# A decoder kernel of two layers: the order of the steps of its first phase laid out anew on all five queues

## The chip, the cores and the metric

The kernel runs on one core of one Trainium2 chip. The time is the device time of one execution in microseconds (us). Before the change the median of three runs is 4827.91 us (4826.06 to 4829.62).

## The reference, cut to what matters

The input is x of shape 64 x 128 x 256 (64 sequences of 128 tokens) in float32, with a context of the same shape and two masks. Six blocks are added to x one after the other:

```
x = x + mamba(layernorm(x))                      # phase 1, chains M, V and N
x = x + cross_attention(layernorm(x), ctx, mask) # phase 1, chains Y and X
x = x + moe(layernorm(x))                        # shared part and router: phase 1, chain F
x = x + causal_attention(layernorm(x))           # phase 3
x = x + perceiver_attention(ctx, layernorm(x))   # phase 3
x = x + ternary_linear(layernorm(x))             # phase 3
```

Inside the mamba block the state recursion over 128 tokens with 32 heads is computed in closed form: with a cumulative sum c of A times dt over the tokens, head h needs the 128 x 128 matrix exp(c[t,h] - c[s,h]) times the masked product of B and C, and multiplies it with the tokens' values. The differences c[t,h] - c[s,h] of eight heads at a time are what the chain N calls "diff".

## The kernel before, in words

**Phases.** Phase 1 runs over the 64 sequences and does the first two blocks, the router and the shared part of the third. Phase 2 runs the 144 expert tiles. Phase 3 runs over the 64 sequences again and does the rest. The change touches phase 1 alone.

**Chains and steps.** In phase 1 the work is written as chains: M (first layer norm, dt, softplus series, cumulative sum), V (projections, convolution, gates) on sequence n, N (differences, exponentials, products with the state, output projection) on sequence n-1, Y and X (context keys and values, cross attention) on sequence n-2, F (router, shared expert, scatter) on sequence n-3. One body of the loop advances every chain by one sequence. Each chain is a Python generator on each engine and is cut into named steps by `yield`. The name of a step in the order is the chain's letter and the step's name: `Nd0` is step d0 of chain N.

**Order.** `ORDER[1]` lists for each of the five queues (SP, POOL, DVE, ACT, PE) in what order the steps of one body are issued. Nothing else orders them: every engine works strictly through its list, and waits (`done`) and reuse waits (`was`) on semaphores stand inside the steps. The buffers are single, so a step may not run before the reader of the same buffer in the body before has finished. A name that is listed but isn't a step of that engine (such as `Vgz` on PE) would be an error, so both orders hold the same steps.

**The steps that the prediction speaks of**, with their lines:

- On POOL (GpSimd): `Nd0` to `Nd3` (L618) subtract the per-token sums `cums` from the rows `Ew[j]`, 128x1024 each, in place. `Nm3` (L622) multiplies the fourth with the masked product `cbm`. `Mln1`, `Xln2`, `Fln3` (L582 to L585) are four instructions on 128x1 for the layer norms. `Msp` (L594 to L610) is thirteen small instructions for softplus; the last gives `a`. `Xx1r` (L635), `Nyg` (L625), `Nrms` (L628, L629), and `Fsc` (L646), which issues two scatter DMAs.
- On ACT (ScalarE): `Ng0` to `Ng3` (L1199) take the absolute value, `Ne0` to `Ne3` (L1202) the exponential. `Mln1`, `Xln2`, `Fln3` (L1145) normalise, `Mln1n`, `Xln2n`, `Fln3n` (L1137) copy the transposes out. `Mab` (L1171, L1173), `Frx` (L1257), `Vbc` (L1184), `Vxp` (L1187), `Xq` (L1241), `FhT` (L1263), and `Mcum` (L1178, L1179), which copies the cumulative sums to `cums` and `cumT`.
- On DVE (VectorE): `Nm0` to `Nm2` (L847) multiply the first three with `cbm`. `Ftop` (L893 to L905) is the top two of the router, `Fslot` (L908 to L912) the rows' places, `Msp` (L802 to L804) what POOL's `Msp` waits for, `Vcv` (L817) and `Vcv1` to `Vcv3` (L819) the convolution, `Ny0` and `Ny1` (L852) the state products' sum with the skip, `Xm0` to `Xm3` the maxima of the scores, `Xho` (L784, L785, L880) the heads' output, and bn_stats and bn_aggr (L754, L755) in `Mln1`, `Xln2`, `Fln3`.
- On PE (TensorE): `Mln1n`, `Xln2n`, `Fln3n` (L1402) transpose, `Fr` (L1390) the router's logits, `Vbc`, `Vip1`, `Vip1h`, `Xq` (L1390) projections, `Frk` (L1561, L1562), `Fgu` and `Fguh` (L1397), `Xs0` and `Xs2` (L1521, L1419), `Nv0` to `Nv3` (L1488), `Fdn` (L1390), `Mcum` (L1446, L1447), then the tail: `Xt0` to `Xt3`, `Vz`, `Xpv0` to `Xpv3`, `XOT`.
- On SP (SyncE, DMA issues): `Mco` (L437) stores `cumT` in memory, `Ncb0` to `Ncb3` (L446) fetch it back as eight heads' rows for all partitions, 512 KB each. `Ncb0` waits for the store of the body before. `Yc`, `Xm`, `Mx`, `Nx` fetch inputs, `Fm` (L464) and `Fo` (L467) store.

So one ring runs from body to body: `Mcum` (PE) makes the sums, `Mcum` (ACT) copies them, `Mco` (SP) stores them, `Ncb0` fetches them, `Nd0` (POOL) of the next body starts, and later in that body POOL's `Msp` makes the `a` for the next `Mcum`.

The waits of the ring in the code:

```
if j == 0:
    done(sp, "cum_out", b, 16)          # Ncb0 on SP
was(sp, "Yk", b, j + 1)
...
done(pool, f"wide{j}", b, 16)           # Nd0 to Nd3 on POOL
...
done(pool, "ratio", b)                  # Msp on POOL, for DVE's Msp
...
done(pe, "a", b)                        # Mcum on PE
```

Of the kernel before, what the change touches and what calls it, by code (L numbers as in the profile page):

```python
# [47 lines left out]
ORDER = {  # L48
    1: {
        "SP": """  # L50
            Ncb0 Ncb1 Ncb2 Yc Xm Mx Ncb3 Nx Mco Fm Fo
        """,
        "POOL": """
            Nd0 Nd1 Nd2 Xx1r Fln3 Xln2 Mln1 Nd3 Msp Nm3 Fsc Nyg Nrms
        """,
        "DVE": """
            Fln3 Xln2 Nm0 Mln1 Fr Yk Ftop Mdt Fslot Msp Xm0 Xm1 Fhg Nm1 Nm2 Xm2 Xm3 Fxo Vcv Vcv1 Vcv2 Vcv3 Ny0 Vxs2 Ny1 Vcb Vxdt Vgz Nx1 Xho
        """,
        "ACT": """
            Ng0 YcT Ne0 Ng1 Fln3 Xln2 Fln3n Xmr Xln2n Mln1 Frx Mln1n Xq Mab Vbc Ne1 Ng2 Yv Fth Ne2 Ng3 FhT Ne3 Xm0 Xm1 Vxp Xm2 Mcum Xm3 NYt0 Xt0 NYt1 Xt1 Vcth Xt2  # L60
            Xt3 Nsq XOT NyT Vtz
        """,
        "PE": """
            YcT Yk Nv0 Fln3n Yv Xln2n Fr Mln1n Xq Vbc Mdt Frk Xs0 Fgu Fguh Vip1 Vip1h FhT Xs2 Fdn Mcum Nv1 Nv2 Xt0 Nv3 Xt1 Ny0 Xt2 VCB Ny1 Xt3 Xpv Xpv0 VxsT Xpv1
            Xpv2 NyT Xpv3 Vz Vzh Npr Nprh XOT
        """,
    },
    3: {
# [1752 lines left out]
```

How the kernel before makes its waits and increments, by code:

```python
        def done(eng, name, b, k=1):  # L124
            eng.wait_ge(SEM[name], at(name, b, k))
# [1 line left out]
        def was(eng, name, b, k=1):  # L127
            if not isinstance(b, int) or b > 0:
                eng.wait_ge(SEM[name], at(name, b, k) - PER[name])
# [202 lines left out]
        def link(eng, name, b, ins, bare=False):  # L333
            steps[name] += 1
            assert steps[name] <= links[name], name
            ins.then_inc(SEM[f"link_{name}"], 1)
            eng.wait_ge(SEM[f"link_{name}"], at(f"link_{name}", b, steps[name]))
            if bare:
                eng.sem_inc(SEM[f"passed_{eng.engine.name}"], 1)
# [28 lines left out]
        def met(eng, me, k):  # L369
            eng.sem_inc(SEM[f"phase_{me}"], 1)
            for other in ("PE", "DVE", "ACT", "POOL"):
                if other != me:
                    eng.wait_ge(SEM[f"phase_{other}"], k)
# [18 lines left out]
        @block.sync  # L393
# [67 lines left out]
            def F(b):  # L461
                yield "m"
                done(sp, "slot", b)
                tell(sp.dma_start(rows(slot_d, b), meta[:, :]), "meta_out", 16)
                yield "o"
                done(sp, "xo", b)
                tell(sp.dma_start(rows(x2_d, b), xo), "xo_out", 16)
            program(sp, "SP", 1, (("M", M, 0), ("N", N, 1), ("Y", Y, 2), ("X", X, 2), ("F", F, 3)))
            sp.wait_ge(SEM["plan"], 1)
            sp.dma_start(routed_d[SPARE:SPARE + P, :], zero).then_inc(SEM["tails"], 16)
            zeros_behind(sp, range(NE // 2))
            sp.wait_ge(SEM["scattered"], at("scattered", NB, 0))
```

## Time and profile before

| | |
|---|---|
| median of three runs | 4827.91 us |
| the profiled execution's own time | 4827.89 us |
| its span, first to last instruction | 4826.3 us |
| PE busy | 4224.3 us (88%) |
| DVE busy | 3368.1 us (70%) |
| ACT busy | 2909.1 us (60%) |
| POOL busy | 2734.9 us (57%) |
| mean granted clock of TensorE | 0.923 of full |

Busy shares are means over three phases of different kinds. Phase 1 reaches to about 2430 us, phase 2 to about 2850 us, phase 3 to the end. A granted clock of 1.00 is 2.4 GHz, 0.50 is 1.2 GHz. PE rows give matmuls, PEld rows weight loads beside them; SPq rows are DMA issues. A float32 matmul shows as two records.

### The profile page before, as it was taken

The numbers are of one execution on the slowest core, as the hardware profiler recorded it, in microseconds if no ns is written. First come the engines' busy times: TensorE is split into PE (matmuls) and PEld (weight loads), VectorE is DVE, ScalarE is ACT, GpSimd is POOL, SyncE is SP. The second block draws the span as 40 slices with busy tenths as digits, with TensorE's granted clock in tenths as the row PEclk, the third lists the DMA queues.
The fourth block names the chain that finished last, engine by engine and source line by source line (L and its number), as shares of the span: only waits on it lengthen the run. The fifth ranks groups of instructions, "written<-read, shape, count | busy, mean of one in ns | idle before, by whom it ended". The sixth has DMA issues, their size and how long they took to land.

```text
span 4826.3 us, 119218 instructions
## 1 busy us (share of the span) xinstructions
PE 4224.3 (88%) x33430; PEld 3093.7 (64%) x33431; DVE 3368.1 (70%) x8668; ACT 2909.1 (60%) x7030; POOL 2734.9 (57%) x4093
## 2 busy tenths in 40 slices
PE   3788888888888888888869979999999999999998
PEld 2666666666666666666647756666666666666665
DVE  2776677666776667766745547777777777777776
ACT  2666666666666666666634436666666666666564
POOL 3666666666666666666622235555555555555554
PEclk9888888888888888888979989999999999999998
DMA  5222222222222222222214411111111111111110
GB/s 155 72 82 90 74 74 74 89 83 74 74 78 92 75 74 74 83 88 75 74 59 145 144 39 31 30 31 31 31 29 31 30 31 31 31 31 31 31 31 18
DMA packets 215885, 304.09 MB, mean 63 GB/s; under 512 B 56608, under 2 KB 167456, under 8 KB 215840
## 3 DMA queue, kind: packets, MB, share of 16 engines
q1 hardware_dynamic: 188864, 240.33, 16.0%
q0 software_dynamic: 19200, 52.45, 3.3%
q10 hardware_dynamic: 7776, 10.75, 0.7%
q8 instruction: 23, 0.38, 0.0%
q14 instruction: 22, 0.18, 0.0%
HBM read 239.19 MB, written 64.23 MB: 63 GB/s over the span
## 4 chain that ended last, share of the span: by engine, by line
PE 51%; POOL 20%; issue 17%; DVE 6%; ACT 2%; POOLq 1%; SPq 1%; DMA 0%; DVEq 0%; ACTq 0%
PE Q L1397 14%; PE Q L1402 8%; POOL arena L618 7%; PE Q L1390 6%; PE Q L1488 4%; PE Q L1425 3%; PE Q L1735 3%; PE Q L1768 3%; PE Q L1589 3%; PE Q L1434 2%; POOL arena L625 2%; PE Q L1601 2%; POOL arena L605 1%; PE Q L1419 1%; POOL arena L606 1%
## 5 line engine op out<-in xcount | busy, mean ns | idle before, releaser
L1402 PE MATMUL Q<-ident,arena 128*128 128x128 f32 x4768 | 801.5, 291 | 148.7 <-ACT arena L1145 35.3
L1402 PEld LDWEIGHTS Q<-ident,arena 128*128 128x128 f32 x4768 | 557.0, 145 | 388.2 <-issue 123.7
L1397 PE MATMUL Q<-Wkvl,arena 128*128 128x512 f32 x1024 | 500.3, 601 | 0.0
L618 POOL TENSOR_TENSOR arena<-arena 128x1024 f32<-128x1024 f32 x256 | 479.4, 1889 | 7.2 <-DMA arena<-cum_rows 7.2
L682 POOL TENSOR_TENSOR l<-l,half_pow 128x8 f32<-128x8 f32 x192 | 318.5, 1659 | 233.2 <-DVE l L1025 231.3
L707 POOL TENSOR_TENSOR arena<-arena,part_of 128x512 f32<-128x512 f32 x256 | 263.7, 1041 | 190.8 <-DVE part_of L1063 190.4
L1488 PE MATMUL Q<-arena 128*16 128x128 f32 x4096 | 223.6, 339 | 169.1 <-DVE arena L847 167.9
L769 DVE TENSOR_REDUCE mx<-Q 128x4 f32<-128x512 f32 x512 | 343.9, 681 | 10.2 <-PE Q L1419 5.5
L1425 PEld LDWEIGHTS Q<-ident,arena 128*128 128x128 f32 x2048 | 244.2, 148 | 116.5 <-issue 84.9
L1425 PE MATMUL Q<-ident,arena 128*128 128x128 f32 x2048 | 314.0, 288 | 1.3 <-ACT arena L1155 0.4
L1155 ACT ACTIVATE arena<-Q,mx 128x128 f32<-128x128 f32 x1024 | 281.8, 372 | 0.7 <-DVE mx L769 0.5
L1419 PE MATMUL Q<-arena 32*128 32x128 f32 x4096 | 278.7, 274 | 0.0
L1162 ACT ACTIVATE arena<-Q 128x512 f32<-128x512 f32 x384 | 222.0, 597 | 83.2 <-PE Q L1425 79.1
L1488 PEld LDWEIGHTS Q<-arena 128*16 128x16 f32 x4096 | 129.4, 107 | 222.2 <-DVE arena L847 169.0
L1202 ACT ACTIVATE arena<-arena 128x1024 f32<-128x1024 f32 x256 | 268.4, 1048 | 0.1
L1199 ACT ACTIVATE arena<-arena 128x1024 f32<-128x1024 f32 x256 | 268.3, 1048 | 0.0
L1419 PEld LDWEIGHTS Q<-arena 32*128 32x128 f32 x4096 | 261.4, 188 | 3.6
L1361 ACT ACTIVATE arena<-Q,mxl 128x256 f32<-128x256 f32 x512 | 235.4, 472 | 45.0 <-DVE mxl L1058 37.6
L1390 PEld LDWEIGHTS Q<-arena,Win 128*128 128x128 f32 x1536 | 235.8, 235 | 33.5 <-issue 29.2
L1434 PE MATMUL Q<-arena 128*17 128x128 f32 x4096 | 208.1, 276 | 41.4 <-ACT arena L1162 41.4
L1390 PE MATMUL Q<-arena,Win 128*128 128x128 f32 x1536 | 236.9, 315 | 3.1 <-ACT arena L1184 2.2
L1397 PEld LDWEIGHTS Q<-Wkvl,arena 128*128 128x128 f32 x1024 | 170.3, 191 | 104.2 <-issue 104.0
(310 smaller groups left out, 10753.3 us busy)
## 6 DMA issues: line engine op xcount, KB each, us to landing
arena<-cum_rows SPq DMA_DIRECT2D x256, 512.0 KB, 6.1
arena<-routed_rows SPq DMA_DIRECT2D x144, 128.0 KB, 2.1
expert_rows<-arena POOLq DMA_DIRECT2D x144, 128.0 KB, 2.0
arena<-in_x_dram SPq DMA_DIRECT2D x128, 128.0 KB, 4.4
arena<-in_ctx_dram SPq DMA_DIRECT2D x128, 128.0 KB
x_rows<-arena SPq DMA_DIRECT2D x128, 128.0 KB, 1.7
arena<-x_rows SPq DMA_DIRECT2D x128, 128.0 KB, 2.3
out_dram<-arena SPq DMA_DIRECT2D x64, 128.0 KB, 1.7
```

The lines of the kernel that those rows point to most:

```text
L618: tell(g.tensor_tensor(E8[j], E8[j], cums[:, 8 * j:8 * j + 8].unsqueeze(2).broadcast_to([P, 8, T]), ALU.subtract), "diff")
L682: link(pool, c, b, g.tensor_tensor(l2[:, k, :], l2[:, k, :], half_pow[:, :], ALU.pow), bare=True)
L769: largest = v.tensor_reduce(mx[:, 4 * j:4 * j + 4], pj, AX.X, ALU.max, negate=True)
L1155: last = s_.activation(S[:, j, g, :], banks[j][:, g * T:(g + 1) * T], ACT.Exp, bias=mx[:, 4 * j + g:4 * j + g + 1])
L1202: tell(s_.activation(Ew[j], Ew[j], ACT.Exp, scale=-1.0), "E")
L1390: last = mm(out, lhs(c), rhs(c), start=c == 0, stop=c == n - 1)
L1397: last = mm(out, lhs(c), rhs(c), start=c == 0, stop=c == n - 1)
L1402: last = nc.tensor.transpose(out[:, c * P:(c + 1) * P], src[:, c * P:(c + 1) * P], ident[:, :])
L1419: last = mm(banks[j][:, g * T:(g + 1) * T], QT[r, g, :], KT[r, g // 2, :], start=False, stop=g == NG - 1)
L1425: last = nc.tensor.transpose(bank[:, g * T:(g + 1) * T], S[:, j, g, :], ident[:, :])
L1434: last = mm(bank[32 * (h % 4):32 * (h % 4) + AW + 1, h // 4 * T:(h // 4 + 1) * T], V[:, h, :], PT[:, j, g, :], start=True, stop=True)
L1488: last = mm(Q[3 + j // 2][32 * (i % 4):32 * (i % 4) + HP, (h // 4 % 4) * T:(h // 4 % 4 + 1) * T], xdt[:, h * HP:(h + 1) * HP], E8[j][:, i, :],
```

## The change

Only the lists of phase 1 change. No step is added or removed, and no step's own code changes; the same instructions are issued in another order on each of the five queues.

- SP: `Fm` (the store of the rows' places) moves ahead of `Mco`.
- POOL: `Nd3` moves up to stand right behind `Nd0`, `Nd1`, `Nd2`; then come `Xx1r`, `Mln1`, `Fln3`, `Xln2`. `Nm3` moves ahead of `Msp`, `Nyg` ahead of `Fsc`.
- DVE: `Mln1` first; `Nm1` and `Nm2` move up; `Ny0` and `Ny1` move up, in between `Xm0` and `Xm1`; the convolution moves up ahead of the score maxima and is cut in two halves; `Nx1` ahead of `Vxdt`, `Xho` last.
- ACT: `Ng0`, `Ne0` to `Ne3` and the norms are interleaved anew, `NYt0`, `NYt1` and `Nsq` move up, `Yv` moves down.
- PE: `Mln1n`, `Mdt`, `Nv1` move up, `VCB`, `Nv2`, `Nv3`, `Ny0`, `Ny1` too, `NyT` and `Npr`; `Xs2` moves down behind `Mcum`, and the tail becomes `Xt0 VxsT Xt1 Xt2 Vz Vzh Xt3 Xpv ... XOT`.

```diff
     1: {
         "SP": """
-            Ncb0 Ncb1 Ncb2 Yc Xm Mx Ncb3 Nx Mco Fm Fo
+            Ncb0 Ncb1 Ncb2 Yc Xm Mx Ncb3 Nx Fm Mco Fo
         """,
         "POOL": """
-            Nd0 Nd1 Nd2 Xx1r Fln3 Xln2 Mln1 Nd3 Msp Nm3 Fsc Nyg Nrms
+            Nd0 Nd1 Nd2 Nd3 Xx1r Mln1 Fln3 Xln2 Nm3 Msp Nyg Fsc Nrms
         """,
         "DVE": """
-            Fln3 Xln2 Nm0 Mln1 Fr Yk Ftop Mdt Fslot Msp Xm0 Xm1 Fhg Nm1 Nm2 Xm2 Xm3 Fxo Vcv Vcv1 Vcv2 Vcv3 Ny0 Vxs2 Ny1 Vcb Vxdt Vgz Nx1 Xho
+            Mln1 Fln3 Nm0 Xln2 Yk Nm1 Mdt Nm2 Fr Ftop Fslot Msp Vcv Vcv1 Xm0 Fhg Ny0 Ny1 Xm1 Fxo Vcv2 Xm2 Vcv3 Xm3 Vxs2 Vcb Nx1 Vxdt Vgz Xho
         """,
         "ACT": """
-            Ng0 YcT Ne0 Ng1 Fln3 Xln2 Fln3n Xmr Xln2n Mln1 Frx Mln1n Xq Mab Vbc Ne1 Ng2 Yv Fth Ne2 Ng3 FhT Ne3 Xm0 Xm1 Vxp Xm2 Mcum Xm3 NYt0 Xt0 NYt1 Xt1 Vcth Xt2
-            Xt3 Nsq XOT NyT Vtz
+            Ng0 Ne0 YcT Ng1 Ne1 Ng2 Mln1 Ne2 Mln1n Ng3 Fln3 Ne3 Fln3n Mab Frx Xln2 Vbc Xmr NYt0 Vxp Xln2n Xq Fth NYt1 Xm0 FhT Nsq Mcum Xm1 Yv NyT Xm2 Vcth Xm3 Xt0
+            Xt1 Xt2 Vtz Xt3 XOT
         """,
         "PE": """
-            YcT Yk Nv0 Fln3n Yv Xln2n Fr Mln1n Xq Vbc Mdt Frk Xs0 Fgu Fguh Vip1 Vip1h FhT Xs2 Fdn Mcum Nv1 Nv2 Xt0 Nv3 Xt1 Ny0 Xt2 VCB Ny1 Xt3 Xpv Xpv0 VxsT Xpv1
-            Xpv2 NyT Xpv3 Vz Vzh Npr Nprh XOT
+            YcT Yk Yv Nv0 Mln1n Mdt Nv1 Fln3n Fr Vbc Xln2n Vip1 Vip1h Frk VCB Xq Fgu Fguh Xs0 Nv2 Nv3 Ny0 Ny1 FhT Fdn Mcum Xs2 NyT Npr Nprh Xt0 VxsT Xt1 Xt2 Vz
+            Vzh Xt3 Xpv Xpv0 Xpv1 Xpv2 Xpv3 XOT
         """,
     },
```

## Rows read from the trace of the kernel before

**Rows 1.** The page, part 1: busy us, share of the span, instructions
```profile
PE 4224.3 (88%) x33430; PEld 3093.7 (64%) x33431; DVE 3368.1 (70%) x8668; ACT 2909.1 (60%) x7030; POOL 2734.9 (57%) x4093
```

**Rows 2.** Instructions of one line, L629, which runs once in each body
```profile
L629 POOL TENSOR_TENSOR ss<-ss,half_pow x61: 567/567/572, 175.4 to 2427.2; 128x1 f32<-128x1 f32 x61
```

**Rows 3.** Timeline of POOL in one body: start us, us, engine line, what
```profile
1039.24 5.59 POOL L618 TENSOR_TENSOR arena<-arena 128x1024 f32<-128x1024 f32 x3
1045.53 0.73 POOL L635 TENSOR_TENSOR arena<-arena,bv0b 128x256 f32<-128x256 f32 x1 [0.69 <-DVE arena L880]
...
1058.85 0.24 POOL L594 TENSOR_TENSOR arena<-arena 128x32 f32<-128x32 f32 x1 [6.12 <-DVE arena L804]
...
1062.25 1.20 POOL L605 TENSOR_TENSOR arena<-arena 128x32 f32<-128x32 f32 x1 [0.34 <-POOL arena L602]
...
1066.18 0.26 POOL L610 TENSOR_TENSOR arena<-arena,Aneg 128x32 f32<-128x32 f32 x1 [0.18 <-POOL arena L609]
1066.40 2.41 POOL L622 TENSOR_TENSOR arena<-arena 128x1024 f32<-128x1024 f32 x1
```

**Rows 4.** Timeline of ACT in the same body
```profile
1048.37 0.60 ACT L1145 ACTIVATE arena<-arena,mvF 128x256 f32<-128x256 f32 x1 [2.04 <-POOL mvF L585]
...
1057.78 1.05 ACT L1202 ACTIVATE arena<-arena 128x1024 f32<-128x1024 f32 x1
...
1067.98 0.25 ACT L1179 ACTIVATE arena<-Q 32x128 f32<-32x128 f32 x1
```

**Rows 5.** Timeline of SP's queue, end of that body
```profile
1068.39 0.35 SPq L437 DMA_DIRECT2D cum_rows<-arena  x1
...
1071.06 1.33 SPq L446 DMA_DIRECT2D arena<-cum_rows  x3
```

**Rows 6.** Landings of L446's later fetches, bodies from 1108.6 and 1146.1
```profile
DMA to landing us min/median/max: 6.0/6.5/7.0
...
DMA to landing us min/median/max: 4.6/5.2/5.7
```

**Rows 7.** Timeline of DVE in the same body
```profile
1052.98 0.17 DVE L893 RECIPROCAL rt<-rt 128x1 f32<-128x1 f32 x1
...
1055.73 0.14 DVE L905 TENSOR_SCALAR meta<-rt 128x1 f32<-128x1 f32 x1
...
1062.13 2.41 DVE L847 TENSOR_TENSOR arena<-arena 128x1024 f32<-128x1024 f32 x2
...
1065.99 3.23 DVE L817 SCALAR_TENSOR_TENSOR arena<-arena,convw,convb 128x128 f32<-128x128 f32 x4
1069.25 3.55 DVE L819 SCALAR_TENSOR_TENSOR arena<-arena,convw 128x128 f32<-128x128 f32 x12
```

**Rows 8.** Timeline of PE in the same body
```profile
1054.73 1.75 PE L1390 MATMUL Q<-arena,Win 128*128 128x128 f32 x8
...
1056.82 0.39 PE L1521 MATMUL Q<-mrow,mask_w 32*128 32x512 f16 x2
...
1058.08 1.98 PE L1397 MATMUL Q<-Wsgu,arena 128*128 128x512 f32 x4
1059.90 1.95 PE L1390 MATMUL Q<-arena,Win 128*128 128x128 f32 x16
...
1063.85 1.13 PE L1390 MATMUL Q<-Wsd,arena 128*128 128x256 f32 x4
1066.49 0.64 PE L1446 MATMUL Q<-arena,triu 128*128 128x32 f32 x2 [1.51 <-POOL arena L610]
...
1070.14 0.63 PE L1488 MATMUL Q<-arena 128*16 128x128 f32 x16
```

**Rows 9.** Stages: start:end us, busy us of each engine, granted clock, DMA
```profile
1046.00:1048.20 2.20, 0.00 (x0) 0.00 (x0) 1.89 (x6) 0.33 (x1) 1.80 (x5) 1.00 0.01 2
1049.00:1056.00 7.00, 6.68 (x28) 6.10 (x29) 2.73 (x16) 3.79 (x11) 3.42 (x7) 0.53 0.00 0
...
1066.70:1069.50 2.80, 2.80 (x37) 1.85 (x38) 2.77 (x3) 1.61 (x7) 2.63 (x2) 0.50 0.02 6
```

## The prediction

> **What bounds the kernel now.** I read the page first, then one line's instructions for the loop's pace, then the timeline of one body engine by engine, then the stages with their clock. On the page no engine is full over the whole span [rows 1], which says little, since three phases are mixed. The pace says more: L629 runs once in a body, its 61 instructions lie between 175.4 and 2427.2 us [rows 2], so a body of phase 1 takes (2427.2 - 175.4)/60 = 37.53 us. The median of the runs (4827.91) and the profiled execution (4827.89) are one number here, and the span lies 1.6 us below it, so a sum over bodies can be added to either.
>
> In one body the reader should see a ring. With POOL's first difference at 1039.24 as zero: ScalarE's `Fln3` starts at 9.1 [rows 4]; POOL waits 6.1 us for VectorE's L804 and starts `Msp` at 19.6; its last instruction L610 ends at 27.2 [rows 3]; TensorE waited 1.5 us for just that and makes the sums [rows 8]; ScalarE's copy L1179 ends at 29.0 [rows 4]; the store is issued at 29.15, the first fetch at 31.8 [rows 5], and the next body starts at 37.5. No engine is full; each waits for another once or twice around the ring. So the place to read this change is when `cumT` is copied, counted from the body's first difference.
>
> Two things in this body stretch it. **The clock:** with no matmul from 1046.0 to 1048.2, TensorE then runs at 0.53 for 7 us (0.50 is 1.2 GHz), and again at 0.50 after the wait of 1.5 us ahead of `Mcum` [rows 8, 9]. Sixteen 128-column records take 1.95 us at 2.4 GHz, eight take 1.75 at 1.2 [rows 8]. **VectorE and POOL hold each other up:** POOL's L605, 128x32, takes 1.20 us (its sisters L609 and L610 some 0.26) while VectorE's L847 runs; POOL's L622 takes 2.41 where L618 of the same shape takes 5.59/3, and in that time VectorE's four L817 take 3.23 us where twelve L819 take 3.55 [rows 3, 7]. Each has two operands in SBUF. They take turns, an instruction at a time.
>
> **The change, part by part.** Nothing is added or removed, so each term is a move. All times below are after `Nd0`.
>
> 1. POOL: four differences take 4 x 1.87 = 7.5 us instead of 5.6, then `Xx1r` 0.7: 8.2. The fetches come 1.3 us apart at best (512 KB at the 400 GB/s they reach, an estimate from the landings in [rows 6]), so the fourth is in time.
> 2. `Mln1` on POOL is the next thing ScalarE needs. Uncontended it is 1.3 us, done at 9.5. But VectorE finishes the body before only at about 6.3 (step 7), runs two bn_stats pairs (0.7 each), and then `Nm0`, 1.2 us [rows 7], from 7.75 to 9.0, with both operands in SBUF. I charge 0.75 us: 10.2. The two other norms meet `Nm1` and `Nm2` in the same way.
> 3. ScalarE is in order: `Mln1` 0.6, `Ne2` and `Ng3` about 0.95 each in a row (1.05 shown, starts 0.94 apart [rows 4]), with the copy `Mln1n` between: `Fln3` starts at 12.95 instead of 9.1. This is what the row of differences costs: `Ng3` stands ahead of `Fln3`.
> 4. From there `Ne3` (0.95) stands ahead of the copy `Fln3n`, done 14.75; then the logits at the low clock (0.9, half of `Vbc`'s eight records), maximum and exponential 0.7 with the hand-offs (an estimate, by the small instructions of 0.2 to 0.3 in [rows 3, 7]), done 16.4, `Ftop` 2.9 us (1052.98 to 1055.87 [rows 7]) and 0.3 for a collision with POOL's `Nm3`: 19.6.
> 5. `Frk` stands behind `Vbc` and the two `Vip1`. `Vbc` costs 1.75 at 1.2 GHz [rows 8]; ScalarE's copy lets `Vip1` start at 18.0; it takes 1.95 us at 2.4 GHz, 3.5 at 1.2. TensorE has four gaps of about 1 us between 9.5 and 15, so I let the clock be low until about 18.5: `Vip1h` ends 20.5, `Frk` 20.7, then `Fslot` 1.0 and VectorE's `Msp` 0.8. POOL's `Msp` starts at 22.5, against 19.6. It no longer meets L847: 7.55 us less 0.95 and 0.75 is 5.85. Now it meets `Vcv` and `Vcv1` instead, eight operations of 0.3; I add 0.75: `a` at 29.1, against 27.2.
> 6. But TensorE isn't there. Behind `Frk` it does `VCB` (after ScalarE's 0.5 copy, 0.9 together), `Xq` 1.15, `Fgu` 1.8, `Xs0` 1.25, `Nv2`, `Nv3`, `Ny0`, `Ny1` 0.57 each with 0.1 of waiting, `FhT`, a copy and `Fdn` 2.0 [rows 8], starts taken one from the next: 20.7 + 9.5 = 30.2. `Mcum` 0.9 and the copies 0.45 end at 31.55. **Term: 31.55 - 29.0 = +2.55 us.** Before, `Mcum` waited for `a`; now it waits for TensorE's own list, and the products and state transposes put ahead of it are 2.4 of that.
> 7. The tail: 11.2 us of matmuls behind `Mcum` with waits of about 2 us for the softmax and for `Vxdt` put `XOT` at 44.1 and `Xho` at 45.6, that is 6.3 into the next body: the assumption of step 2. Its cover is thin: if the tail ends 1 us later, `Mln1` on VectorE is late by as much.
> 8. SP: `Fm` ahead of `Mco` is 0.6 us in a queue that waits for `cumT` anyway: nothing. If `Fslot` were later than `cumT` it would cost, but it is 10 us earlier. `Fo` behind `Mco` is issued while SP waits for the store.
> 9. The way through memory. Store and first fetch: 2.8 us from the copy's end [rows 4, 5]. The first fetch's landing is not shown. The second and third land 4.6 to 7.0 us after they are issued [rows 6], and they are issued 0.7 us and more behind the first; taking off the 1.3 us of its successor, the first lands 4.1 to 5.5 us after its issue. So the copy gates the next `Nd0` after 6.9 to 8.3 us; the body before uses 8.5, so it has 0.2 to 1.6 us of slack there. The scatter's transfers end before the fetches now, where they overlapped, so I take the lower half: 7.4.
>
> **The sum:** 31.55 + 7.4 = 38.95 us a body, against 37.53: +1.42. Times 63 bodies from one first difference to the next of 64 sequences: +89 us. 4827.9 + 89 = 4917 us. Phases 2 and 3 don't change. `Nsq`, `NYt0`, `NYt1`, `Yv`, `Nx1`, `NyT` cost nothing by themselves, covered by ScalarE's and VectorE's waits ahead of `Mcum`; if that cover were gone, each is 0.3 to 0.6.
>
> On the clock, the second fall came after a gap of 1.5 us only [rows 8, 9]. The Trainium skill, page "TensorE: Matmul & The Clock Gate", section "HAM oscillation — how this bites in real kernels", says that only a long gap without matmuls brings the clock down; by that rule the gaps of step 5, none of them above 1.3 us, would leave it at 2.4 GHz. Its result is the second rival.
>
> **The rivals.**
>
> - *The clock stays high* (chance 0.12). The gaps of step 5 are short, and TensorE is busy through step 7. Then `Fr` and `Vbc` take half, `Vip1h` ends at 19.4, `Ftop` becomes the later one, and the ring shortens by 1.05: 37.9 us, +23 us, 4851. Against it: 1.5 us sufficed in [rows 8, 9]. The page's rule named above is this case.
> - *Faster: the ring is tight only if both charges fall on it* (0.24). Place: from POOL's `Mln1` to ScalarE's `cumT`. If neither the clock (1.05) nor the turn-taking with `Nm0` (0.75) lies on the ring, `cumT` is copied at 29.75, and with the fetch at its fastest, 7.0, the body is 36.75: -0.78 x 63 = -49, 4779. It decides from a copy that ends before about 30.5. For it: POOL's wait of 6.1 us has gone, the scatter is out of the fetches' way, and `Msp` no longer meets L847. Against it: the ring has little give, since ScalarE alone has six steps ahead of `Fln3n`.
> - *The ring is bound elsewhere, in the same time* (0.10). If `Nd0` is not gated by the fetch but POOL's order again, the moves cancel, 4820 to 4837.
> - *Low clock to the end of `Vip1h`* (0.08). 3.5 us instead of 2.5, and `Nm0` holding up `Nd3` as well: 40.2 us, +168, 4996.
>
> The forecast has what is left, 0.46.
>
> **How the numbers follow.** About 0.2% (10 us) is what a measurement of this kernel can tell from no change. Faster 0.24, within it 0.10, slower 0.46 + 0.12 + 0.08 = 0.66. The unknown costs are the clock (0 to 2 us a body), the turns on SBUF (0 to 1.5) and the landing (6.9 to 8.3); the forecast's own range is 37.9 to 39.8 us, 4851 to 4971. The full range reaches to the faster rival, 4778, and up to 4995.
>
> **What would show it.** Right: L629's spacing near 38.9 us; ScalarE's first L1145 3 to 4 us later behind `Nd0`; POOL's L594 at 22 to 23 and its wait gone to ahead of `Nd0`, put down to `cum_rows` or an issue; TensorE's L1446 no longer waiting for L610; a low clock between 11 and 19. L605 near 0.25, and some of the centre instructions near 1 us beside L847. Wrong: L1446 starting before 28, or L1446 still waiting for L610, or `Nd0` following L629 without idle time, which would say that the ring isn't closed by the memory round trip.

## The result, and the profile after

The changed kernel takes 4888.43 us (median of four runs, 4870.07 to 4907.4), the kernel before 4826.99 (median of four): a ratio of 1.013, with a 95% interval of 1.0086 to 1.0174. It is 61 us slower, where 89 were forecast. The profiled execution is the slowest of the four, 4907.4 us, and lies 79 us above the profiled execution of the kernel before; the numbers of its bodies and rings below are from that trace. One run of a later kernel (5030.45 us, in "All together") lies over 1.5% above the fastest of its kernel, at a lower clock, and is left out of that kernel's median.

Page of the changed kernel, parts 1 and 4 (shares of the chain that ended last):

```profile
PE 4195.5 (86%) x33430; PEld 3034.8 (62%) x33431; DVE 3296.0 (67%) x8668; ACT 2914.5 (59%) x7030; POOL 2744.1 (56%) x4093
...
PE 72%; ACT 11%; issue 8%; DVE 4%; POOL 2%; DMA 2%; SPq 1%; DVEq 0%; ACTq 0%; POOLq 0%
```

The same line of the kernel before:

```profile
PE 51%; POOL 20%; issue 17%; DVE 6%; ACT 2%; POOLq 1%; SPq 1%; DMA 0%; DVEq 0%; ACTq 0%
```

POOL had 20% of the last chain; now it has all but left it. The loop's pace, the row that answers to [rows 2]:

```profile
L629 POOL TENSOR_TENSOR ss<-ss,half_pow x61: 567/567/574, 178.7 to 2497.2; 128x1 f32<-128x1 f32 x61
```

(2497.2 - 178.7)/60 = 38.64 us a body, against 37.53. The mean hides something that the kernel before doesn't have. The bodies of that one, from one first difference to the next, are nearly all alike: 55 of the 56 from the fifth to the sixtieth are under 37.8 us and none is over 38.5. Of the same 56 of the changed kernel 21 are under 37.8, near 37.55, and 29 are over 38.5, up to 40.6.

Timeline of POOL, one body of the changed kernel of 40.6 us (start us, us, what, then idle time before it and who ended it), answering to [rows 3]:

```profile
1033.42 5.61 POOL L618 TENSOR_TENSOR arena<-arena 128x1024 f32<-128x1024 f32 x3 [3.85 <-DMA arena<-cum_rows]
...
1042.55 0.73 POOL L635 TENSOR_TENSOR arena<-arena,bv0b 128x256 f32<-128x256 f32 x1 [1.12 <-DVE arena L880]
...
1050.24 2.35 POOL L622 TENSOR_TENSOR arena<-arena 128x1024 f32<-128x1024 f32 x1 [0.45 <-ACT arena L1202]
1059.27 0.28 POOL L594 TENSOR_TENSOR arena<-arena 128x32 f32<-128x32 f32 x1 [6.68 <-DVE arena L804]
...
1062.93 0.25 POOL L605 TENSOR_TENSOR arena<-arena 128x32 f32<-128x32 f32 x1 [0.34 <-POOL arena L602]
...
1065.14 0.25 POOL L610 TENSOR_TENSOR arena<-arena,Aneg 128x32 f32<-128x32 f32 x1 [0.18 <-POOL arena L609]
```

`Nd0` now stands idle 3.85 us for its fetch; in [rows 3] and [rows 5] POOL went from one body into the next without a wait. The wait of 6 us ahead of L594 has stayed. L605, 1.20 us in [rows 3], takes 0.25, now that VectorE's L847 doesn't run beside it.

Timeline of ACT, then of SP's queue, then of PE, in the same body, answering to [rows 4, 5, 8]:

```profile
1039.76 0.60 ACT L1247 ACTIVATE arena<-Q 128x512 f32<-128x512 f32 x1 [0.72 <-PE Q L1434]
1040.25 1.05 ACT L1199 ACTIVATE arena<-arena 128x1024 f32<-128x1024 f32 x1
...
1048.54 0.59 ACT L1145 ACTIVATE arena<-arena,mvF 128x256 f32<-128x256 f32 x1
...
1067.49 0.25 ACT L1179 ACTIVATE arena<-Q 32x128 f32<-32x128 f32 x1
```

```profile
1067.90 0.35 SPq L437 DMA_DIRECT2D cum_rows<-arena  x1
...
1069.84 1.58 SPq L446 DMA_DIRECT2D arena<-cum_rows  x3
```

```profile
1050.41 1.03 PE L1390 MATMUL Q<-Wr,arena 128*128 128x16 f32 x4 [0.78 <-ACT arena L1137]
1051.28 2.06 PE L1390 MATMUL Q<-arena,Win 128*128 128x128 f32 x8
...
1053.80 3.52 PE L1390 MATMUL Q<-arena,Win 128*128 128x128 f32 x16
...
1066.57 0.30 PE L1446 MATMUL Q<-arena,triu 128*128 128x32 f32 x2
```

ScalarE's work on the differences starts at 1040.25, right behind `XOT` of the tail (L1247), though POOL's first difference ended near 1035.3. `Fln3` starts 15.1 us behind `Nd0` (mean of the bodies 14.0), where it was 9.1. L1446 no longer waits for L610: over 114 records the view of that line names no idle time. In the kernel before it named this, over 118 records:

```profile
  POOL arena L610: 202.3, 118
```

`Vip1` and `Vip1h` take 3.52 us where they took 1.95, at the low clock.

Stages (start:end us, us, busy us of PE, PEld, DVE, ACT, POOL, clock, DMA), answering to [rows 9]:

```profile
1049.50:1053.00 3.50, 2.72 (x14) 2.60 (x13) 1.01 (x5) 2.05 (x7) 2.64 (x2) 0.58 0.00 0
1053.00:1056.50 3.50, 3.45 (x16) 3.05 (x16) 1.61 (x11) 1.16 (x3) 0.00 (x0) 0.50 0.00 0
1056.50:1067.00 10.50, 9.24 (x90) 6.69 (x88) 8.42 (x25) 4.87 (x12) 5.44 (x15) 0.98 0.01 0
```

For the ring as a whole I took from each trace the starts of a few lines, counted from the end of the copy to `cumT` (L1179) and averaged over 56 bodies:

```
us behind the copy's end      before   after
Nd0 starts (L618)              8.61     6.29
Xho's sum starts (L880)       14.40    14.03
router's maximum (L889)       21.70    22.98
Fslot starts (L908)           26.36    28.27
next copy ends                37.54    38.60
```

From the tail to the router's maximum the new order loses 1.65 us (7.30 to 8.95), on to `Fslot` 0.63, and it wins 0.85 behind that and 0.37 ahead of it: 1.06 in sum.

These are means over rings that differ. From one copy to the next, 22 of the 56 rings of the changed kernel take 37.57 us, as long as in the kernel before (37.54). Sorted by how much of a ring TensorE spent at 1.2 GHz:

```
us at 1.2 GHz   rings   us from copy to copy, mean
3.4             22      37.57
6.8             26      38.92
10.2             2      39.88
13.7             6      40.55
```

One ring each with 3.4, 6.8 and 13.7 us (start:end us, us, busy us of PE, PEld, DVE, ACT, POOL, clock, DMA):

```profile
1608.20:1645.76 37.56, 29.35 (x264) 21.65 (x262) 24.91 (x71) 24.58 (x54) 23.95 (x37) 0.95 0.24 79
1067.74:1106.58 38.84, 30.86 (x264) 22.79 (x262) 24.87 (x71) 24.69 (x55) 23.98 (x37) 0.91 0.21 76
1948.84:1989.34 40.50, 33.65 (x264) 25.20 (x262) 24.59 (x71) 24.81 (x54) 24.32 (x37) 0.83 0.22 73
```

What the other 34 rings take above 37.57 adds up to 58 us, which is nearly the whole loss of this execution's loop. It stands where the further low clock stands: in the tail (`Xho` starts 14.91 us behind the copy in the 16 rings with low clock there, 13.69 in the 40 without), and between `Xho` and `Fslot`.

### The profile page after: what moved, and what is told of

It reads as the page before. It is cut to its first block, busy times and chain, and to the rows that moved or that the text cites. A ratio compares the mean times of both kernels' runs of the same rounds, so it can differ in the third digit from the quotient of the medians.

```text
span 4905.7 us, 119223 instructions
## 1 busy us (share of the span) xinstructions
PE 4195.5 (86%) x33430; PEld 3034.8 (62%) x33431; DVE 3296.0 (67%) x8668; ACT 2914.5 (59%) x7030; POOL 2744.1 (56%) x4093
## 4 chain that ended last, share of the span: by engine, by line
PE 72%; ACT 11%; issue 8%; DVE 4%; POOL 2%; DMA 2%; SPq 1%; DVEq 0%; ACTq 0%; POOLq 0%
PE Q L1397 21%; PE Q L1390 15%; PE Q L1402 11%; ACT arena L1199 4%; PE Q L1419 3%; PE Q L1434 3%; PE Q L1425 3%; PE Q L1735 3%; PE Q L1768 3%; PE Q L1589 3%; ACT arena L1202 2%; PE Q L1488 2%; PE Q L1601 1%; DMA arena<-cum_rows 1%; POOL arena L618 1%
## 5 line engine op out<-in xcount | busy, mean ns | idle before, releaser
L1402 PE MATMUL Q<-ident,arena 128*128 128x128 f32 x4768 | 801.0, 289 | 183.5 <-ACT arena L1145 45.8
L1402 PEld LDWEIGHTS Q<-ident,arena 128*128 128x128 f32 x4768 | 543.4, 144 | 443.5 <-issue 145.7
L618 POOL TENSOR_TENSOR arena<-arena 128x1024 f32<-128x1024 f32 x256 | 480.3, 1900 | 272.2 <-DMA arena<-cum_rows 270.9
L1390 PE MATMUL Q<-arena,Win 128*128 128x128 f32 x1536 | 318.5, 384 | 3.8 <-ACT arena L1184 0.9
L1425 PEld LDWEIGHTS Q<-ident,arena 128*128 128x128 f32 x2048 | 246.4, 143 | 114.6 <-issue 101.0
L1390 PEld LDWEIGHTS Q<-arena,Win 128*128 128x128 f32 x1536 | 290.0, 287 | 30.0 <-ACT arena L1184 29.2
L1425 PE MATMUL Q<-ident,arena 128*128 128x128 f32 x2048 | 282.1, 276 | 3.4 <-ACT arena L1155 2.4
L1361 ACT ACTIVATE arena<-Q,mxl 128x256 f32<-128x256 f32 x512 | 235.4, 472 | 45.0 <-DVE mxl L1058 37.6
L819 DVE SCALAR_TENSOR_TENSOR arena<-arena,convw 128x128 f32<-128x128 f32 x768 | 238.6, 372 | 2.4
L847 DVE TENSOR_TENSOR arena<-arena 128x1024 f32<-128x1024 f32 x192 | 235.2, 1225 | 2.2 <-ACT arena L1202 2.2
L1397 PE MATMUL Q<-Wout,arena 128*128 128x256 f32 x512 | 158.2, 463 | 86.4 <-ACT arena L1214 85.7
```

What stands on the lines that cost most here:

```text
L618: tell(g.tensor_tensor(E8[j], E8[j], cums[:, 8 * j:8 * j + 8].unsqueeze(2).broadcast_to([P, 8, T]), ALU.subtract), "diff")
L1390: last = mm(out, lhs(c), rhs(c), start=c == 0, stop=c == n - 1)
L1397: last = mm(out, lhs(c), rhs(c), start=c == 0, stop=c == n - 1)
L1402: last = nc.tensor.transpose(out[:, c * P:(c + 1) * P], src[:, c * P:(c + 1) * P], ident[:, :])
L1425: last = nc.tensor.transpose(bank[:, g * T:(g + 1) * T], S[:, j, g, :], ident[:, :])
```

## The experiments

Twelve kernels were run, each in turns with the kernel before on the same chip; the ratio is to that. The changed kernel itself was not run again beside them. Its four runs spread over 37 us, so a difference to its 4888.43 us says little when it is below about 25 us. Times inside a body are of the profiled execution.

**A longer way through memory, in the changed kernel.** The edit, on SP in `Ncb0`, with an array `again_d` beside `cum_d`:

```diff
 done(sp, "cum_out", b, 16)
+tell(sp.dma_start(rows(again_d, b), cumT[0:NH, :]), "again", 16)
+done(sp, "again", b, 16)
```

> The changed kernel with a second store of cumT, to another array, issued and waited for on SP between the first store and the first fetch: about 2 us more on the way through memory in each body. Theory M (of the prediction: the ring is closed by the memory round trip, since POOL's Nd0 stands idle 3.9 us for cum_rows in a body): +2 us x 63 = +126 us, about 5015. Theory R (read in the trace after: the ring runs through the in-order lists of TensorE and ScalarE, Ng0 on ScalarE starts only behind the body before's XOT, 6.8 us after Nd0 starts, so 4.9 us of the trip are slack): within 20 us of the changed kernel's 4888.

It took 5019.95 us (ratio 1.0401, with the 95% interval 1.0384 to 1.0419), 132 over the changed kernel. Theory M's 5015 was met, though partly by luck: it charged 2 us a body, and the fetch came only 1.5 later. The first fetch was issued 3.6 us behind the copy instead of 2.1, the first difference started 7.7 behind it instead of 6.3, and a body took 40.48 us instead of 38.60. Theory R, read straight from the chain of waits, fell. `Ng0` starts late, and so the chain doesn't name POOL, but POOL's four differences end at 6.29 + 7.76 = 14.05 us behind the copy, and `Xho`, the other thing that `Xx1r` waits for, ends at 14.65 on the mean, and later than the fourth difference in all 56 bodies. Two rings of nearly one length meet at `Xx1r`; the chain of waits shows the later one. They are also tied by more than that wait. `Xho`'s sum L880, 0.43 us in the kernel before, takes up to 1.6 in the changed kernel and up to 2.2 with the longer way, when POOL's L618 runs beside it. So of the delay of 1.40 us ahead of `Nd0` 1.26 reach `Xx1r`. The body grew by 1.88, since the low clock rose too, from 6.3 us a body to 10.1.

**The same in the kernel before.**

> The kernel before with the same second store and wait on SP ahead of the first fetch: the fetch is issued 1.5 us later, as the trace of the first such run shows. The changed kernel took 132 us for it. If the kernel before is closed through memory just as tightly, as the prediction had it with 0.2 to 1.6 us of slack: 0 to 80 us, somewhere near the middle (+40). If it has the whole slack that the trace of the changed kernel lets one expect (a first fetch lands 4.2 us after its issue there, so 7.0 after the copy, against 8.6 used): under 15 us. As much as the changed kernel, 100 us or more: then the memory ring is no difference between the two.

4833.7 us, 1.0012 (1.0002 to 1.0022), 8 us. Here the first fetch was issued 5.1 us behind the copy instead of 2.8, a longer delay than in the changed kernel, but `Nd0` started only 0.5 later (9.1 behind the copy instead of 8.6). The idle time of POOL (its waits between 200 and 2300 us: us in total, times, longest) of the changed kernel, of the changed kernel with the longer way, and of the kernel before with the longer way:

```profile
POOL arena L618 <- DMA arena<-cum_rows: 226.7, 80, 4.3
```

```profile
POOL arena L621 <- DMA arena<-cum_rows: 302.7, 96, 5.8
```

```profile
POOL arena L621 <- DMA arena<-cum_rows: 39.8, 78, 1.1
```

So the kernel before had about 1.8 us of slack in its memory ring, and the changed one has next to none: of its 1.5 us, 1.4 reached `Nd0`. This is the sharpest difference between the two: one edit, 8 us in the one and 132 in the other.

**ScalarE's norms ahead of its row.** In the changed kernel's ACT list:

```diff
-Mln1n Ng3 Fln3 Ne3 Fln3n Mab Frx
+Mln1n Fln3 Ng3 Fln3n Mab Ne3 Frx
```

> The changed kernel with two swaps on ScalarE: Fln3 ahead of Ng3, and Fln3n and Mab ahead of Ne3. Theory R: the chain of waits has Ng3 (1.05 us) and Ne3 (0.95) ahead of the router's logits, so a body is up to 1.9 us shorter, less what POOL's Fln3 (done 0.9 us earlier than ScalarE takes it) and the later Nm3 give back: -1 us x 63, about 4825. Theory M, with the row of differences as the cost: the same sign, through cumT, but no less idle time of POOL ahead of Nd0.

4912.0 us (1.0189, 1.017 to 1.0208), where 4825 was expected: a miss. It is 24 above the changed kernel's median, but the two profiled executions are alike (4905.5 and 4907.4 us, a body 38.64 and 38.60), so what is shown is that nothing was gained. `Ne3` later makes POOL's `Nm3` later (17.1 us behind `Nd0` instead of 15.7) and POOL's `Msp` behind it too (24.1, 23.8 before the edit). `Fln3` itself came only 0.4 us earlier (13.6 behind `Nd0`).

**VectorE's `Msp` early.** In the changed kernel's DVE list:

```diff
-Nm2 Fr Ftop Fslot Msp Vcv
+Nm2 Fr Msp Ftop Fslot Vcv
```

> The changed kernel with VectorE's Msp ahead of Ftop instead of behind Fslot: POOL's Msp can start some 6 us earlier and a is ready some 5 us earlier. Theory R: Mcum on TensorE is held by TensorE's own list (it starts 1.2 us after a is ready), so nothing moves but POOL's idle time: within 20 us of 4888. Rival (POOL's Msp still on the ring, or its turns with the convolution on SBUF cost VectorE): 1 us a body or more, under 4825.

4895.18 us (1.0151, 1.0134 to 1.0168), 7 over the changed kernel and inside its spread. `a` was ready at 24.8 us behind `Nd0` instead of 30.0, and `cumT` was copied at 32.2 instead of 32.3. POOL's wait of 6 us, the longest in its view, was worth nothing.

**The row undone.** In the changed kernel's lists of POOL and ACT, all else as changed:

```diff
-Nd2 Nd3 Xx1r Mln1 Fln3 Xln2 Nm3
+Nd2 Xx1r Mln1 Fln3 Xln2 Nd3 Nm3
...
-Mln1n Ng3 Fln3 Ne3 Fln3n Mab Frx Xln2 Vbc Xmr NYt0
+Mln1n Fln3 Fln3n Mab Frx Xln2 Ng3 Vbc Xmr Ne3 NYt0
```

> The changed kernel with the row of differences undone: POOL's Nd3 back behind the three norms, and ScalarE's Ng3 and Ne3 behind Fln3n, Frx and Xln2. Theory T (two rings are tied within 0.7 us at POOL's Xx1r: the memory trip with four differences, and TensorE's tail with Xho; behind it the norms wait for the row and for Ng3 and Ne3): the router's maximum comes 1.3 to 1.9 us earlier behind Xho, a body is about 1 us shorter, 4888 - 63 = about 4825, the time of the kernel before. Rival (as ScalarE's two swaps alone, which gave 4912: what ScalarE gains there, POOL's Msp loses behind the later Nm3): 4880 to 4920.

4838.41 us (1.0017, 1.0008 to 1.0027): 50 of the 61 us are back. From copy to copy all 56 rings are alike, 37.56 us on the mean, each with 6.8 us of low clock, always between `Xho` and the end of `Vip1` and never in the tail. So undoing the row took away the long rings; against the changed kernel's 22 rings of 37.57 us it won nothing. On the means the pieces moved like this: the tail is 1.2 us shorter (`Xho` starts 12.84 behind the copy), from `Xho` to the router's maximum it is 8.47 us instead of 8.95, on to `Fslot` 5.92 instead of 5.29, where the low clock now always lies, and 10.33 behind that in both. `Fln3` starts 12.2 us behind `Nd0` instead of 14.0, and 1.3 of these 1.8 us are the earlier `Xho`. The part for which step 3 blamed the row, `Ng3` ahead of `Fln3`, is thus 0.5 us.

Of the 1.2 us in the tail the clock explains only 0.3, since the changed kernel's rings with a high clock throughout it stand at 13.69. The rest shows right behind the copy. `NyT` (PE's L1402) starts 0.6 us behind it in both kernels, at the high clock, but ScalarE's L1214, which waits for it, starts 1.3 us behind the copy in all rings here and 2.0 in 55 of 56 of the changed kernel. Two rows of the changed kernel (copy at 724.09), two of this one (copy at 698.28):

```profile
724.69 0.66 PE L1402 MATMUL Q<-ident,arena 128*128 128x128 f32 x4
726.07 0.60 ACT L1214 ACTIVATE arena<-Q 128x512 f32<-128x512 f32 x1 [1.20 <-PE Q L1402]
...
698.89 0.66 PE L1402 MATMUL Q<-ident,arena 128*128 128x128 f32 x4
699.58 0.60 ACT L1214 ACTIVATE arena<-Q 128x512 f32<-128x512 f32 x1 [0.52 <-PE Q L1402]
```

What holds it up there is not shown.

**`Mcum` early as well.** To the early `Msp` comes, on PE and ACT of the changed kernel:

```diff
-Xs0 Nv2 Nv3 Ny0 Ny1 FhT Fdn Mcum Xs2
+Xs0 Mcum Nv2 Nv3 Ny0 Ny1 FhT Fdn Xs2
...
-Xq Fth NYt1 Xm0 FhT Nsq Mcum Xm1
+Xq Fth Mcum NYt1 Xm0 FhT Nsq Xm1
```

> The changed kernel with VectorE's Msp ahead of Ftop (alone: 4895, no change) and Mcum on TensorE directly behind Xs0, on ScalarE behind Fth: cumT is copied some 5 us earlier, and the first fetch is issued when Fo lets it, 2 to 2.5 us earlier. Theory T: the memory ring gets slack, but TensorE's list is as long and Xho as late, 0.5 to 0.7 us are left to gain by POOL's Xx1r, 4845 to 4880, and POOL's idle time for cum_rows shrinks from 4 us to about 2. Theory M (memory ring alone): -2 us x 63, 4760.

4859.06 us (1.0054, 1.0037 to 1.0071), 29 under the changed kernel, in the interval of theory T. The copy ended at 28.2 us behind `Nd0`, 4.1 earlier, but the first fetch was issued at 33.4, 1 us earlier only, since on SP it stands behind `Fo`, which waits for `xo`. The low clock, 7.0 us a body, lies outside the tail in nearly every ring, as with the row undone; 53 of the 56 rings take 37.58 us on the mean. How much of the 29 us is the clock and how much the earlier `Mcum` is not separated.

**Extra matmuls in front of waits.** A helper on PE writes to a part of a bank that nobody reads then, in front of the waits of `Yk`, `Mdt`, `Fr`, `VCB`, `Npr` and `Vz`:

```diff
+def fill(n, bank=4):
+    for _ in range(n):
+        mm(Q[bank][:, 0:64], ident[:, :], ones[:, 0:64], start=True, stop=True)
...
+fill(3)
 done(pe, "ln1_T", b)
```

> The changed kernel with three extra 128x64 float32 matmuls in front of each of six waits of TensorE (Yk, Mdt, Fr, VCB, Npr, Vz), into a bank that nobody reads then, to keep TensorE busy. Theory: the bodies of 39 to 40.6 us are those with 7 to 14 us at 1.2 GHz, those of 37.6 have 3.4 us; with the clock high all the time a body is 36.5 to 37.5 us: -1.2 us x 63, about 4810, and no body over 38. Rival (the clock is a companion of the longer waits, not their cause, or the extra matmuls cost more than they hide): 4888 or slower.

4840.95 us (1.0028, 1.0016 to 1.0041): 47 less than the changed kernel, with eighteen matmuls more. 47 of 56 bodies are under 37.8 us, three over 38.5; low clock is 3.3 us a body instead of 6.3, and none of it in the tail. Nothing but TensorE's activity was changed, so the clock makes the long bodies; it doesn't just go with them. And the row of differences still stands in this kernel: undoing the row brought back 50 us and keeping the clock up 47, so the two are not separate costs. The row costs mainly through the low clock. How the order brings the clock down more often is not shown.

**More of them.**

> The changed kernel with more extra matmuls than the 18 of the run at 4841 (29 in nine places): there every body had one stretch of 3.4 us at 1.2 GHz, 16 us after Nd0, and took 37.5; the six bodies without it took 37.0. If the clock is what is left: no low stretch, 36.9 us a body, about 4800. If the extra matmuls cost as much as they give: 4841 or slower.

4862.64 us (1.0063, 1.0035 to 1.0091, runs from 4845 to 4883): the second half of the expectation. But the bodies tell more than the median. 36 have no low clock at all and take 36.84 us, 17 have 10 us of it and take 40.43. The same instructions in the same order, 3.6 us apart with nothing but the clock to tell them apart. What tips a body over I can't say.

**The same on the kernel before**, nine ahead of `Nv0`'s wait and six ahead of `Mcum`'s:

> The kernel before with nine extra 128x64 float32 matmuls ahead of Nv0's wait and six ahead of Mcum's, where it stands idle 2.6 and 1.5 us and then has 6.8 and 3.4 us at 1.2 GHz in every body. If the low clock is on its ring: 1.5 to 2.5 us a body, 4670 to 4735. If its ring runs through POOL, VectorE and the memory trip with TensorE's matmuls beside them: under 30 us gained, or none.

4824.21 us (0.9983, 0.9973 to 0.9993), 6 us under the kernel before in the same rounds. The expectation's second half fits the median. The trace doesn't fit it: it is of the fastest of the ten runs, 4803.58 us, 24 us under the profiled execution of the kernel before, and its low clock fell from 9.8 to 3.8 us a body. In it 12 of the 56 rings have no low clock and take 35.58 us, 26 have 3.4 us of it and take 37.26, and 18 have 6.8 and take 38.14. Two in a row, one with 6.8 us and one without (start:end us, us, busy us of PE, PEld, DVE, ACT, POOL, clock, DMA):

```profile
946.12:984.25 38.13, 33.01 (x297) 25.16 (x289) 26.34 (x69) 24.21 (x55) 24.61 (x37) 0.91 0.26 78
984.25:1019.52 35.27, 30.24 (x297) 23.86 (x289) 25.88 (x73) 24.31 (x55) 22.91 (x36) 1.00 0.26 84
```

So the low clock does lie on the ring of the kernel before, 1.7 us for the first 3.4, and a version of it that kept the clock up in every body would be some 2 us a body faster than it is (an estimate from these rings, 35.58 against 37.54). The extra matmuls did that in one ring of five; in the others they moved the low clock into the tail, 6 to 10 us behind the copy, where it costs. This is the only version of the twelve with an interval under the kernel before, by an amount below the 0.2% that I set as the bound.

**All together**, the row undone, `Msp` and `Mcum` early, and on POOL `Msp` ahead of `Nm3`; without extra matmuls, and with 25 of them:

> The row undone (alone 4838) together with VectorE's Msp ahead of Ftop and Mcum behind Xs0 (together alone 4859, 29 under the changed kernel), and POOL's Msp ahead of Nm3. Theory: both rings get shorter, the two gains of 50 and 29 us add: about 4809, or more than that since cumT is copied some 3 us before the tail needs it. Rival (both only took away the same 0.7 us at POOL's Xx1r, and the low clock of 6.8 us in each body holds the pace at 37.55): 4825 to 4840.

> The same with 25 extra 128x64 float32 matmuls ahead of eight waits of TensorE. In the row undone alone every body has 6.8 us at 1.2 GHz, in which Vbc and both Vip1 run in 5.6 us instead of 3. If they are on the ring and the extra matmuls keep the clock up: 2 us a body less, about 4690 to 4710, under both kernels. If the clock falls in some bodies all the same, as in the run at 4863: around 4780 and a wide spread.

4960.12 us (1.0282, 1.0257 to 1.0307) and 4845.1 (1.0037, 1.0023 to 1.0051). Both expectations failed, the first on the other side. Two causes show in the trace of the first. One is the clock: 27 bodies without low clock take 37.5 us, and eleven with 15 us of it take 42.9. The other is in these pieces of the chain of waits of a body without low clock (start us, us, what):

```profile
1301.45 1.14 DVE arena L802
1302.62 0.36 DVE arena L803
...
1307.37 1.15 DVE arena L817 x4
...
1308.54 3.34 DVE arena L819 x4
```

and in POOL's timeline beside it:

```profile
1300.65 1.89 POOL L618 TENSOR_TENSOR arena<-arena 128x1024 f32<-128x1024 f32 x1
...
1309.32 2.40 POOL L622 TENSOR_TENSOR arena<-arena 128x1024 f32<-128x1024 f32 x1
```

L802, 128x32, is 0.19 us in the changed kernel and 1.14 here, behind POOL's L618, which ends at 1302.54. `Vcv1`, four L819 in 1.46 us in the changed kernel, takes 3.34, one of the four 2.45, while POOL's `Nm3` runs. Moved together the steps put both collisions, 2.8 us, on the chain of waits. With the 25 extra matmuls the clock is 1.00 in the loop and a body is 37.56 us, the two collisions still in it. Whether `Nm3` ahead of `Msp` would have brought this version under the kernel before was not tried.

**The row undone with the extra matmuls.**

> The row undone alone with the same 25 extra matmuls: tells whether Msp and Mcum early matter once the clock is up. If the memory ring is then the tighter one: about 0.5 to 1 us a body more than with them, 4720 to 4760. If not: the same time.

4851.96 us (1.005, 1.0036 to 1.0065), 14 slower than without them. The clock is high in nearly the whole loop, and still the tail is 1.3 us longer (`Xho` 14.15 us behind the copy instead of 12.84). Part of that may be the extra matmuls in it; ScalarE's L1214 also starts late again, 2.5 to 2.6 us behind the copy instead of 1.3 in 51 of 56 rings. The two were not separated. Against the version with all moves and the same extra matmuls it is 7 us slower, with intervals that overlap: that fits the second half of the expectation, "the same time", though both times lie above the 4690 to 4760 that were expected.

## Why the prediction was right, point by point

The direction and the range were right, and the size was 1.4 times too large. The sum came near for the wrong reasons. In the 22 rings without further low clock the copy ends 31.30 us behind `Nd0`, 2.4 later than before (2.55 forecast), and `Nd0` starts 6.27 behind the copy, 2.3 earlier than before (1.1 forecast): 37.57 us, and nothing lost. The loss is the further low clock in the other 34 rings, which the sum, with its one low stretch of the same cost in every body, doesn't have. With the memory leg as measured it would have come to 31.55 + 6.27 = 37.82 us a body, some 18 us for the kernel. That the time fell near the forecast is in good part luck.

- **The sum to the copy** (step 6): forecast 31.55 us behind `Nd0`, measured 32.31 on the mean and 31.30 in the 22 rings. `Mcum` held by TensorE's own list: right, it starts 1.2 us behind the end of `a` and names no wait, and with `a` 5 us earlier nothing moved.
- **The tail** (step 7): from copy to `XOT` and `Xho` 45.6 - 31.55 = 14.05 forecast to its end, 14.65 measured.
- **The way through memory** (step 9), the mis-sized term: forecast 7.4 us from copy to `Nd0`, measured 6.29. The first fetch is issued 2.1 us behind the copy where it was 2.8: `Fm` ahead of `Mco`, which step 8 put at nothing, left only `Fo` between store and fetch. It lands about 4.2 behind its issue, against some 4.6 in the sum. So `Nd0` starts earlier than the tail allows anything to follow, `Xho` ends 8.4 us into the body instead of 6.3, and step 2 starts late. The ring is not closed by memory alone, as step 9 has it; it is tied between memory and tail within 0.6 us. A memory leg of the forecast's length would not have given the forecast's body: with the longer way it was 7.7 us, and a body took 40.48.
- **The row of differences** (step 3) as the main cost: right that it is what loses, as undoing it brings back 50 of 61 us, but not by the way step 3 has it. `Fln3` starts 14.0 us behind `Nd0` (12.95 forecast, 9.1 before), of which 2 us are the late `Xho`; with the row undone it still starts at 12.2, and 0.5 us is the row's own part. The 22 rings have the whole row and lose nothing. The row costs where it comes with more low clock.
- **The clock** (step 5): low, but from about 16 us to 19.4 or 22.4, not from 11 to 18.5, and in 16 of 56 rings in the tail as well. I charged 1 us to every body. In truth 22 rings pay nothing against the kernel before, 26 pay 1.35 us on the mean and the rest 2.3 to 3. The rival in which the clock stays high is refuted for the changed kernel, whose largest gap on TensorE is 1.56 us. Its forecast of 37.9 didn't hold either: with the extra matmuls the rings without low clock take 36.9 and 36.7. The rule that the prediction takes from the page "TensorE: Matmul & The Clock Gate" of the Trainium skill, section "HAM oscillation — how this bites in real kernels", is one on long gaps without matmuls. It didn't hold here: the body of the rows above, with no gap over 1.4 us, had three stretches at 1.2 GHz, and the measurement decides.
- **The turns on SBUF**: `Msp` on POOL at 6.1 us instead of 7.6, forecast 6.6. VectorE's `Vcv` and `Vcv1` together take 2.6 us. The 0.75 us between `Nm0` and POOL's `Mln1` came to 0.5: POOL's four instructions take 1.85 us in every body, of which the last takes 0.69 instead of 0.19 in the body shown.
- **The signs**: a body 38.64 us (38.9 forecast), POOL idle ahead of `Nd0` for `cum_rows`, L1446 without a wait for L610 and L605 at 0.25 us came as foretold. L594 came at 23.8, not 22 to 23, its wait of 6 us was not gone but stayed beside the new one, `Fln3` came 4.9 us later and not 3 to 4, and the low clock lay later than 11 to 19.
- **The rival of the other side** needed the copy before 30.5 us; it came at 32.3 on the mean and 31.1 at the earliest.

With the row undone and all the rest in place, the state products early among it, the kernel stands at 1.0017 of the kernel before, 8 us. That is what the rest costs without the row; what it costs beside the row no run shows.

## What to carry to other kernels

When a step moves up, ask for each queue what then stands behind it: here one 1.9 us instruction on GpSimd and its two on ScalarE went ahead of the norms on which the next stage waits, and undoing that brought back most of the loss. But look at single bodies before you name the cost. The mean body hid that 22 of 56 lost nothing and the others lost by TensorE's clock, and eighteen extra matmuls brought back as much as undoing the move. Two rings of nearly one length hide each other in a chain of waits, which shows only the later; a delay put in on purpose, in both kernels, tells what slack each has. And gains of single moves do not add: two moves worth 50 and 29 us, together with one more, were 122 slower than the better of them.

## What the runs showed of the hardware

- TensorE's clock fell although no gap in the changed kernel's loop was over 1.56 us, and identical bodies took 36.84 us without and 40.43 with 10 us of low clock. Extra matmuls in front of waits kept it up and won 47 us in the one kernel (26 with more of them) and 6 in the other, and lost 14 in a third.
- The kernel before spends more of its loop at 1.2 GHz than the changed one (9.8 against 6.3 us a body) and is faster: it matters where the low clock lies. The page "TensorE: Matmul & The Clock Gate" of the Trainium skill, section "Terms", counts the penalty as the low time's missing share of clock. By that 3.4 us cost 1.7 (an estimate from the page), and in the kernel before with extra matmuls they did, 37.26 us against 35.58. But rings of 37.5 to 37.6 us have 10.2 us of low clock in the kernel before, 6.8 with the row undone and 3.4 in the changed kernel.
- VectorE and GpSimd take turns by whole instructions when both have two operands in SBUF: 128x128 in 2.45 us instead of 0.34, 128x32 in 1.14 instead of 0.19, and 128x256 (L880) in up to 2.2 instead of 0.43.
- Several versions with different orders and clocks settle near 37.5 us a body: the kernel before, the row undone, the eighteen extra matmuls, the changed kernel's own 22 rings, and the high-clock bodies of the version with all moves, without and with extra matmuls. Others take 36.84 and 35.58, so it is no floor. I have no explanation that a run shows.
